# A turned up product: two layers of attention and feed-forward on one core, its hidden tile made already transposed

## The reference

```python
logits = jnp.einsum('bsh,he->bse', hidden_states, gate_w)          # 8 experts
routing_weights, selected_experts = jax.lax.top_k(logits, K)        # K = 2
h = jax.nn.relu(jnp.einsum('bsh,hi->bsi', hidden_states, up_w)) ** 2   # 512 -> 1024
shared_out = jnp.einsum('bsi,ih->bsh', h, down_w)                   # 1024 -> 512
...
return _layernorm(shared_out + routed_out, ln_gamma, ln_beta)
```

## Time and profile before

| | us |
|---|---|
| median of 3 runs (693.44 to 694.46) | 694.11 |
| the profiled execution, its own time | 690.39 |
| its span, first to last instruction | 688.6 |
| TensorE busy | 658.7 (96%) |
| VectorE busy | 495.7 (72%) |
| ScalarE busy | 421.8 (61%) |
| GpSimd busy | 373.4 (54%) |
| mean busy share of the DMA queue q1 over 16 engines | 26.6% |

### The profile page before, as it was taken

One profiled execution on the slowest core, in us unless ns is written; L12 is line 12 of the kernel. 1 busy time (PEld: TensorE's weight loads), 2 busy tenths in 40 slices (PEclk: granted clock), 3 DMA queues, 4 the chain that ended last, 5 costly groups with the idle time before them and its releaser, 6 DMA issues.

```text
span 688.6 us, 12434 instructions
## 1 busy us (share of the span) xinstructions
PE 658.7 (96%) x3898; PEld 477.8 (69%) x3898; DVE 495.7 (72%) x1123; ACT 421.8 (61%) x773; POOL 373.4 (54%) x461
## 2 busy tenths in 40 slices
PE   8789999999989997999999999999999999999986
PEld 3345555555556576788787787887878878787775
DVE  4778888888876777777677776776777767775444
ACT  4668787868647785674755746658367574664221
POOL 1648898987766524445455354553454544534351
PEclk9999999999999999999999999999999999999999
DMA  7333435453134431122212212123021220211000
GB/s 258 101 99 109 151 125 148 129 164 105 61 108 113 135 115 37 48 54 58 74 31 61 64 58 61 38 53 91 30 61 50 66 67 30 61 31 47 16 16 31
DMA packets 32118, 54.36 MB, mean 79 GB/s; under 512 B 5296, under 2 KB 7088, under 8 KB 32080
## 3 DMA queue, kind: packets, MB, share of 16 engines
q1 hardware_dynamic: 32080, 53.90, 26.6%
HBM read 36.84 MB, written 8.39 MB: 66 GB/s over the span
## 4 chain that ended last, share of the span: by engine, by line
PE 83%; DVE 10%; issue 3%; ACT 2%; POOL 1%; POOLq 0%; DVEq 0%; ACTq 0%
PE ps_b L1246 7%; PE wide L1246 7%; PE ps_b L1248 7%; PE ps_b L1247 7%; PE wide L1248 6%; PE wide L1247 6%; PE bank L1358 4%; PE ps_b L1291 4%; PE wide L1348 4%; PE ps_a L1291 4%; PE ps_b L1430 4%; PE ps_a L1246 2%; PE ps_a L1248 2%; PE ps_a L1247 2%; PE wide L1484 2%
## 5 line engine op out<-in xcount | busy, mean ns | idle before, releaser
L758 POOL TENSOR_TENSOR va<-mv,small 128x1 f32<-128x1 f32 x80 | 15.4, 193 | 156.5 <-DVE mv L1225 79.4
L723 ACT ACTIVATE stage<-wide 128x512 f32<-128x512 f32 x30 | 16.3, 595 | 83.7 <-PE bank L1531 83.7
L844 POOL TENSOR_TENSOR y_l<-y,y_h 128x512 fp32r<-128x512 f32 x16 | 21.9, 1370 | 72.5 <-ACT y_h L631 72.5
L1093 DVE RECIPROCAL y<-ps_b 128x256 f32<-128x256 f32 x32 | 55.9, 1748 | 0.4 <-PE ps_b L1430 0.4
L654 ACT ACTIVATE probs<-wide 128x1024 f32<-128x1024 f32 x32 | 32.8, 1025 | 36.1 <-PE wide L1484 36.1
L1246 PE MATMUL wide<-up_h,t_h 128*128 128x512 f32 x128 | 52.1, 407 | 1.5 <-DVE t_l L1177 1.5
L1248 PE MATMUL wide<-up_h,t_l 128*128 128x512 f32 x128 | 50.9, 397 | 0.0
L1247 PE MATMUL wide<-up_l,t_h 128*128 128x512 f32 x128 | 50.4, 394 | 0.0
L1246 PE MATMUL ps_b<-down_h,ht_h 128*128 128x512 f32 x120 | 49.6, 413 | 0.4 <-DVE ht_l L1165 0.4
L760 POOL TENSOR_TENSOR rs<-va,small 128x1 f32<-128x1 f32 x80 | 44.5, 557 | 6.3
L1248 PE MATMUL ps_b<-down_h,ht_l 128*128 128x512 f32 x120 | 47.1, 393 | 0.0
(11 more groups left out here) (227 smaller groups left out, 2100.5 us busy)
## 6 DMA issues: line engine op xcount, KB each, us to landing
q_stack<-qt_h SPq DMA_DIRECT2D x128, 64.0 KB, 2.0
x_in<-in_x SPq DMA_DIRECT2D x16, 256.0 KB, 2.7
ctx_t<-in_ctx SPq DMA_DIRECT2D x16, 256.0 KB, 2.6
x_res<-in_x SPq DMA_DIRECT2D x16, 256.0 KB, 2.7
x_in<-x_rows SPq DMA_DIRECT2D x16, 256.0 KB, 2.6
ctx_t<-in_ctx_turned SPq DMA_DIRECT2D x16, 256.0 KB, 3.0
x_res<-x_rows SPq DMA_DIRECT2D x16, 256.0 KB, 2.9
out<-stage SPq DMA_DIRECT2D x15, 256.0 KB, 3.0
```

Source lines behind the costliest of these rows:

```text
L1093: dve.reciprocal(y[:, :, b, :], part[:, 1]).then_inc(S["den_s"], 1)
```

## The change

The up product is made turned. The up weights' halves become stationary, 128 columns of them at a time (8 slices, IC), and the turned tile's halves move, 128 columns (the tokens) at a time. The result has hidden features on its partitions and tokens along its columns, the form that the down product wants. So turned_hidden, its semaphore ht_ps and its banks go. Each slice n writes its own 128 columns of `wide`; u_ps is raised after the fourth and the eighth slice. hidden_high and hidden_low read act2 in SBUF and not the transposes in PSUM; hidden_high waits for h_s. On ScalarE the second hidden_high of tile i now stands ahead of relu of tile i + 1, and relu, which overwrites act2, waits for both low halves of tile i (ht_lo).

```diff
             def hidden_high(t, part):
-                act.wait_ge(S["ht_ps"], 2 * t + part + 1)
+                act.wait_ge(S["h_s"], t + 1)
                 if not final(t):
                     wait(act, S["dn_ps"], 2 * t + part)
-                act.activation(ht_of(t, part)[0], ht_bank(t, part), ACT.Copy).then_inc(S["ht_hi"], 1)
+                act.activation(ht_of(t, part)[0], act_of(t)[:, D * part:D * (part + 1)], ACT.Copy).then_inc(S["ht_hi"], 1)
...
                 queries_stacked(i + 3)
+                t = i
+                if live(t) and not final(t):
+                    hidden_high(t, 1)
                 t = i + 1
                 if live(t):
-                    wait(act, *((S["pv_ps"], 2 * NT) if final(t) else (S["ht_ps"], 2 * t)))
+                    wait(act, *((S["pv_ps"], 2 * NT) if final(t) else (S["ht_lo"], 2 * t)))
                     for c in range(2):
                         act.wait_ge(S["u_ps"], 2 * t + c + 1)
                         act.activation(act_of(t)[:, c * D:(c + 1) * D], bank[6 + c], ACT.Relu).then_inc(S["relu_s"], 1)
-                t = i
-                if live(t) and not final(t):
-                    hidden_high(t, 1)
...
                 high, low = ht_of(t, part)
-                dve.tensor_tensor(low, ht_bank(t, part), high.bitcast(F32), ALU.subtract).then_inc(S["ht_lo"], 1)
+                dve.tensor_tensor(low, act_of(t)[:, D * part:D * (part + 1)], high.bitcast(F32), ALU.subtract).then_inc(S["ht_lo"], 1)
...
-            def turned_hidden(t, part):
-                pe.wait_ge(S["h_s"], t + 1)
-                if not final(t):
-                    wait(pe, S["qx_lo"], capped(1, t + 4))
-                for c in range(DC):
-                    done = pe.transpose(cols(ht_bank(t, part), c, P), cols(act_of(t), DC * part + c, P), ident)
-                done.then_inc(S["ht_ps"], 1)
...
                 turned_queries(i + 3)
-                t = i
-                if live(t) and not final(t):
-                    turned_hidden(t, 0)
                 attend(i + 2)
                 t = i + 1
                 if live(t):
                     pe.wait_ge(S["t4_lo"], t + 1)
                     wait(pe, S["probs_s"], capped(2, t + 2))
-                    for n in range(2):
+                    for n in range(IC):
                         for c in range(DC):
-                            w = slice(INNER * c + D * n, INNER * c + D * (n + 1))
-                            last = split_product(bank[6 + n], cols(t4_h, c, P), cols(t4_l, c, P),
-                                                 up_h[:, w], up_l[:, w], c == 0, c == DC - 1)
-                        last.then_inc(S["u_ps"], 1)
+                            w = slice(INNER * c + P * n, INNER * c + P * (n + 1))
+                            last = split_product(wide[:, P * n:P * (n + 1)], up_h[:, w], up_l[:, w],
+                                                 cols(t4_h, c, P), cols(t4_l, c, P), c == 0, c == DC - 1)
+                        if n % DC == DC - 1:
+                            last.then_inc(S["u_ps"], 1)
                     routed_part(t, HALF, D + EXPERTS, bank[4])
...
                 output(i + 2)
-                t = i
-                if live(t) and not final(t):
-                    turned_hidden(t, 1)
                 rough_scores(i + 3, 1)
...
-                if closing(i):
-                    turned_hidden(NT - 1, 0)
                 t = i
                 if live(t) and not final(t):
                     down(t, 1)
                 if closing(i):
-                    turned_hidden(NT - 1, 1)
                     down(NT - 1, 0)
                     down(NT - 1, 1)
```

More of the change, by code:

```diff
@@ L245, in build @@
             t4_ps t4_hi t4_lo u_ps relu_s h_s top_s rw_s rt_out_ps routed_s
-            ht_ps ht_hi ht_lo dn_ps z_s zg_s o_s
+            ht_hi ht_lo dn_ps z_s zg_s o_s
             blank_s const_in dft_loaded first_in merge_in lora_in w0_in gate_in bcast_in stage_in stage_odd_in gate_split
@@ L312, in ht_of @@
             return (q_stack[:, 2 * part, :], q_stack[:, 2 * part + 1, :]) if final(t) else (ht_h[:], ht_l[:])
-        def ht_bank(t, part):
-            return bank[part if final(t) else 5]
         def down_bank(t):
```

## The result

The changed kernel takes 784.22 us (median of 4 runs, 782.66 to 784.92) against 693.93 for the kernel before in the same comparison: the ratio is 1.129, with an interval of 1.125 to 1.133. The forecast was 771, its range 757 to 792. The profiled execution takes 782.66 us, its span is 780.8.

The account below looks back on a forecast made before the run. TensorE, busy for 96% of the span, was taken as the bound; twelve steady turns (57.8) plus 4.65, 5.0, 4.3 and 5.0 made 76.8 us on 694.1, so 771 us, 11% slower, range 757 to 792.

Parts of the forecast that it names:

- Term 1: Up stage: 96 products paced by their weight loads at 0.112 us each, stage 10.85 us, +5.15 a turn.
- Term 2: First four hidden-tile transposes of a turn go from TensorE: -0.53 us a turn.
- Term 3: Second four hidden-tile transposes go but lie under the routed part's wait for x3: counted 0, at most -0.53 us.
- Term 4: Moved waits on ScalarE: later relu delays the guard rows that the scores need, +0.2 us a turn, bounds 0 and 1.1.
- The sum of a turn: A steady second-pass turn: +4.82 us, from 28.0 to 32.8.
- turn -1: Second pass: no transposes to lose, but the longer up stage covers a 0.52 us gap: +4.65 us.
- turn 12: No new context to prepare, so guard rows come right behind relu, late by a further 0.2: +5.0 us.
- turn 13: Loses a 0.37 us gap where the down product waits for the second low half: +4.3 us.
- Turn 14: The 1.53 us gap eats the first transposes; later relu, square and halves cost about what the others give: +5.0 us.
- the fall of the clock: Rival: granted clock falls to 1.2 GHz in the up stages, up to +172 us, 943 us; chance 0.03.
- the first rival: Scores wait for the guard rows by the whole of relu, 1.1 instead of 0.2 in turns 0 to 11: 782 us; chance 0.10.
- the signs of being wrong: Up-product step 0.06 or over 0.125, granted clock under 9 in pass 2, or scores waiting over 0.5 us a turn.

Follow-up runs that it names:

- The swap: Output product moved ahead of the first down part: in the changed kernel 773.81 us (median of six; profiled run 765.07), in the kernel before 695.26 us, ratio 1.001.
- The filler: Changed kernel with eight products of 512 columns put in TensorE's idle time ahead of the last up stage: 770.38 us, ratio 1.108.
- the added idle time: TensorE made to wait for VectorE's first reciprocal ahead of turn 12's up stage: 797.30 us in the changed kernel, 698.64 us in the kernel before.
- the narrow products in the old direction: Kernel before, transposes kept, its up product cut into 96 products of 128 moving columns with a load each: 783.89 us, ratio 1.133.

## Why the prediction was right, and what it missed

**Term 1, right.** Forecast 10.85 a stage and +5.15, measured 10.77 and 10.77 - 5.70 = +5.07. The price d, taken from the loads of another product, was 0.112, and 0.112 was measured. Half the load makes it 0.06, half the columns leave it; so it was right for its reason. The Trainium skill (TensorE: Matmul & The Clock Gate, Back-to-back issue gap) gives 81 ns for a pair of 128 columns; that does not hold for this type here: the measured 112 decides.

**Term 2, a little less.** From the transposes of the normalised tile to the up stage 3.54 (442.84 to 446.38) became 3.10 (512.94 to 516.04): -0.44 instead of -0.53. Attention now starts 0.09 later behind the turned queries than before; in turn 6 it starts at 481.20, and ScalarE's probabilities end at 481.18.

**Term 3, right.** The 0.46 us of waiting for x3 stand in the trace, and output product to routed part takes the same 3.74 us as before. The swap shows both halves of it: worth 0.6 a turn without the transposes, nothing with them.

**Term 4, right in size.** The scores come 0.17 later behind the last down product; from the turned maxima to the end of the scores a turn takes 0.28 longer (6.89 before, 7.17 after), forecast 0.2. That it is the guard rows that are waited for fits their end, but no experiment moved them.

**The sum of a turn, right.** 5.07 - 0.44 + 0 + 0.28 = 4.91, forecast 4.82; the profile gives 58.5 for turns 0 to 11 (forecast 57.8), 4.8 for turn -1 (4.65), 5.1 for turn 12 (5.0), 4.3 for turn 13 (4.3).

**Turn 14, wrong.** This is the term that failed: "+5.0" was +16.25, from the last transposes of a normalised tile to the end of the span (658.73 to 688.6 before, 734.68 to 780.8 after). 9.0 of the 11.2 too many are in the up stage at half the clock, the rest in the products behind it, up to 761.9. The prediction had both parts in hand and didn't put them together: it counted the gap of 1.53 as something that eats the transposes, and gave the fall of the clock 0.03, for all stages or none. The filler (-12.5), the added idle time (the same loss in turn 12) and the narrow products in the old direction (the same loss behind the old gap) show that the gap and the narrow stage do it together. Over all the traces, five of the six stages with 128 columns and a load of 128 that stand behind a gap of 1.5 us or more lost the clock, and all four stages of 512 columns behind such a gap kept it. What decides it in one execution stays open: the profiled run of the swapped order kept the clock with the same gap and the same stage.

**What the prediction read too coarsely.** Against a fall of the clock it set that every slice of the earlier trace rows shows the full level, those of pass 1 too. But a slice is 17 us long there, and a 9 stands for 0.9 or more. In stretches of 4 us the same trace has a fall, behind a gap of TensorE, at products of 512 columns:

```profile
28.59 2.08 PE L1291 MATMUL ps_a<-xn,dft 64*128 64x512 f32 x4 [2.80 <-DVE prod L1039]
...
28.00:32.00 4.00, 3.42 (x9) 1.23 (x9) 2.39 (x20) 2.97 (x4) 0.74 (x2) 0.57 0.65 201
```

The same four products take 1.13 us at 17.52. So the trace of before had already shown a fall of the clock behind a gap, there at other products (64 rows, 512 columns) than those of the up stage.

**The range and the signs.** 784 lies within 757 to 792 partly by luck: without the first rival the range ended at 784, and it was that rival's 11 us that made room. The rival didn't come (0.17 of wait, not 1.1); the 11 us came from the clock in one stage, which the range was said to leave out. And one of the signs of being wrong did appear: the granted clock shows 5 in a slice of pass 2. The other two didn't: the step is 0.11, and no wait of over 0.5 stands ahead of the scores.

**The rest.** 3.3 us of the profiles' difference lie in the first 25 us of pass 1, where no instruction was changed: the two profiled executions met the full clock at different times (the first ten products take 5.96 us in one, 7.63 in the other). The turns of the profiles add up to 58.5 + 4.8 + 5.1 + 4.3 + 16.25 = 89.0; the medians are 90.3 apart, and the last 1.3 are not accounted for.

## What to carry to other kernels

Turning a product to save transposes changes how many weight loads it makes: count loads and moved columns separately, price each from rows where the other is small, and take the larger. A stage of products paced by their loads can lose the clock behind a gap that the same stage of wide products kept it behind here; look for gaps directly ahead of it and put work there. Read the granted clock in stretches of a few us, not in the slices of the page, before a fall is ruled out. Work that seems to be removed for nothing may have been the cover of a wait: check what the next instruction waits for before its time is counted.

## What the runs showed of the hardware that was not expected

- A weight load slows down with the granted clock: at the full level one of 128 columns follows the next every 0.112 us, at the 1.2 GHz level every 0.21 (products with a load each, 749.97 to 750.18), also where only 64 columns move beside it (425.82 to 426.03). The prediction left it open whether only the columns would slow down; twice their 0.06 is 0.12, by estimate next to nothing more than the 0.112 of the load.
- With 64 moving columns and 128 loaded ones the clock fell in every up stage, in fifteen of them with no gap listed ahead. With 128 and 128 it fell behind gaps of 1.54, 1.97 and 2.80 us, and once, in the profiled run of the swapped order, it was kept behind 1.97. With 128 moving columns and 64 loaded ones it was kept behind 1.97, with 512 and 128 behind 1.53 and 2.36.
- Products of 512 columns don't always keep it: in pass 1 of the kernel before, some with 64 rows run at a mean clock of 0.57 (28 to 32 us) behind a gap of 2.80.
